# Layer 1's cross attention: the value products of batches 1 to 7 as seven quarter products, with sums on GpSimd

## What is computed

```python
x = x + _L1_xattn_ref(_layernorm(x, axis=-1), ctx_1024, ctx_1024, ...)

def _L1_xattn_ref(Q, K, V, Wq, Wk, Wv, Wo, pre_g, pre_b, ln_g, ln_b):
    D, H, HD, TEMP = 512, 8, 64, math.sqrt(512)
    Qn = _layernorm(Q, pre_g, pre_b)
    Kn = _layernorm(K, pre_g, pre_b)
    q = (Qn @ Wq).reshape(B, Lq, H, HD)
    k = (Kn @ Wk).reshape(B, Lk, H, HD)
    v = (V @ Wv).reshape(B, Lk, H, HD)
    scores = clip(einsum('bqhd,bkhd->bhqk', q, k) / TEMP, -10000.0, 10000.0)
    A = softmax(scores)
    O = einsum('bhqk,bkhd->bqhd', A, v).reshape(B, Lq, D)
    O = _layernorm(O, ln_g, ln_b)
    return O + gelu(O @ Wo)
```

## Time and profile before

| | us |
|---|---|
| runs of the kernel before | 3535.21, 3537.26, 3544.75 (median 3537.26) |
| the profiled execution, own time | 3539.68 |
| its span | 3537.3 |
| PE busy, share of the span | 3102.5, 88% |
| DVE, ACT, POOL busy | 1225.3, 712.7, 392.0 |
| layer 1's cross attention | about 867 to 1204 of the span |
| one regular body (batch) in it | 1008.50 to 1044.37, 35.87 |

### The profile page before, as it was taken

How to read it: one execution, slowest core, us unless ns; L and a number is a source line. 1 busy time by engine, 2 the same in 40 slices (tenths; PEclk the granted TensorE clock), 3 DMA queues, 4 the chain that set the end, 5 groups by cost and what they waited for, 6 DMA issues and landing times. The chain is left out here.

```text
span 3537.3 us, 43385 instructions
## 1 busy us (share of the span) xinstructions
PE 3102.5 (88%) x17505; PEld 1662.7 (47%) x17505; DVE 1225.3 (35%) x2569; ACT 712.7 (20%) x1365; POOL 392.0 (11%) x386
## 2 busy tenths in 40 slices
PE   8998789997899899999889989889998997666666
PEld 5775543333444444344457565436885652111111
DVE  3775430002344569765341132113554310000000
ACT  2443101101232331111012120103452211000000
POOL 4441010001000000001000000004541000000000
PEclk9998889998999999989999999899999999888878
DMA  3110079998111122221540121982002158999999
GB/s 143 45 33 37 13 306 420 406 421 337 62 71 47 37 61 66 101 84 36 207 175 1 45 108 55 376 353 83 24 24 83 77 238 345 420 419 420 420 419 373
DMA packets 103780, 653.65 MB, mean 185 GB/s; under 512 B 20168, under 2 KB 29384, under 8 KB 40648
## 3 DMA queue, kind: packets, MB, share of 16 engines
q1 hardware_dynamic: 98928, 637.67, 44.8%
q0 software_dynamic: 4160, 13.63, 1.0%
q10 hardware_dynamic: 536, 0.14, 0.0%
HBM read 641.89 MB, written 9.50 MB: 184 GB/s over the span
## 5 line engine op out<-in xcount | busy, mean ns | idle before, releaser
L3075 PE MATMUL banks<-ring,h 128*32 128x512 f32 x1024 | 165.2, 754 | 84.5 <-DMA ring<-in_L_ffn_w 61.1
L3058 PE MATMUL banks<-ring,mine 128*32 128x512 f32 x1024 | 167.5, 701 | 51.4 <-DMA ring<-in_L_ffn_w 51.0
L913 PE MATMUL banks<-ring 128*128 128x256 f32 x784 | 179.9, 381 | 0.0
L1839 PE MATMUL banks<-ring,xT 128*64 128x512 f32 x736 | 167.5, 610 | 11.8 <-DMA ring<-in_L_ffn_Wg 5.5
L504 PE MATMUL banks<-normed_features,first 128*128 128x256 f32 x768 | 168.0, 379 | 1.1 <-ACT normed_features L471 1.1
L3186 DVE COPY mine<-mT 128x32 f32<-128x32 f32 x31 | 5.6, 181 | 448.7 <-PE banks L3058 448.7
L913 PEld LDWEIGHTS banks<-ring 128*128 128x128 f32 x784 | 144.5, 190 | 28.7 <-issue 11.4
L429 POOL TENSOR_TENSOR rstd_pairs<-var_eps_pairs,minus_half 128x4 f32<-128x4 f32 x30 | 30.9, 1029 | 1138.7 <-DVE var_eps_pairs L417 961.2
L504 PEld LDWEIGHTS banks<-normed_features,first 128*128 128x128 f32 x768 | 144.6, 190 | 23.0 <-issue 3.2
L3075 PEld LDWEIGHTS banks<-ring,h 128*32 128x32 f32 x1024 | 26.7, 122 | 194.5 <-DMA ring<-in_L_ffn_w 141.9
L886 PE MATMUL banks<-big 128*128 128x512 f32 x256 | 116.9, 602 | 0.0
(11 more groups left out here) (658 smaller groups left out, 5325.7 us busy)
## 6 DMA issues: line engine op xcount, KB each, us to landing
ring<-in_L_ffn_w SPq DMA_DIRECT2D x256, 1024.0 KB, 27.1
ring<-in_L_ffn_Wd SPq DMA_DIRECT2D x24, 2048.0 KB, 23.1
ring<-in_L_ffn_Wg SPq DMA_DIRECT2D x23, 2048.0 KB, 18.8
ring<-in_L_ffn_Wu SPq DMA_DIRECT2D x23, 2048.0 KB, 20.2
wb<-in_L_ffn_W SPq DMA_DIRECT2D x32, 1024.0 KB, 24.5
first<-in_L_ffn_W SPq DMA_DIRECT2D x16, 1024.0 KB, 19.9
second<-in_L_ffn_W SPq DMA_DIRECT2D x16, 1024.0 KB, 22.0
ctxT<-in_ctxT SPq DMA_DIRECT2D x8, 1024.0 KB, 4.9
```

Source lines behind the costliest of these rows:

```text
L913: ins = pe.matmul(halves(n % 2)[:, r, :], a, x, start=(k == 0), stop=(k == 1))
L1839: ins = pe.matmul(ps[H * side:H * side + H, 2 * kind + half, :], xT[:, p % 2, k, H * own:H * own + H], rows_of(where[(name, slot)], C)[:, ...
L3058: ins = pe.matmul(ps[B4 * q:B4 * q + B4, 0, :], mine[:, e % 2, k, :], w[:, q * 512:(q + 1) * 512], start=(k == 0), stop=(k == C - 1))
L3075: ins = pe.matmul(ps[B4 * q:B4 * q + B4, 2, :], h[:, Q * n + q, :], w[:, q * D:(q + 1) * D], start=(n == 0), stop=(n == Q - 1))
```

## The change

In layer 1 too, the values of batches 1 to 7 are made by seven quarter products. The keys stay as they are. In a body the four key units fill steps 0 and 1; step 2 has quarter products 0 to 3, step 3 has 4 to 6. The four turns of the next context follow products 0, 2, 4 and 5. The sums of the value weights and the three copied products lie in `ring`, the buffer that the scan's weights use later; the sums of the context (`csum`) lie in the stage's own space. SP's wait for the values' last unit becomes one for the last quarter product. GpSimd's order becomes: root 0, root 1, the five weight sums, the five sums of context 1, then in each body the root of context b + 2, its five sums, and the four `offsets`; `add_shift` comes after all of it. The value copies of batches 1 to 7 on DVE become joins. Layers 0 and 3 issue what they issued.

```diff
+    KINDS = (1,) if knorm else (0, 1)
+    TURN_AFTER = (0, 2, 4, 5)
...
         def quarters_of(j):
+            if knorm:
+                return range(4 * (j - 2), min(4 * (j - 2) + 4, 7)) if j >= 2 else ()
...
+        def bank_of(par, n):
+
+            return (n + (par if knorm else 0)) % 2
...
                 if not last:
-                    sp.wait_ge(*(multiplied.at(PROD * b + 1) if split else projected.at(UN * b + UN)))
+                    sp.wait_ge(*multiplied.at(PROD * b + 1))
                     sp.dma_start(ctxT[:, par], m.d["ctxT"][b + 2]).then_inc(*ctx_landed[par].up(16))
                     if knorm:
                         sp.wait_ge(*k_turned.at(C * b + 2 * C))
                         sp.dma_start(extra[:], m.d["ctx"][b + 2]).then_inc(*tok_landed.up(16))
...
             def body(b, par, last, step):
                 if last and par == 1:
                     return
-                offsets(b, 1 - par, 0, step)
-                if not last:
-                    mix_context(b + 2, par, step)
-                offsets(b, 1 - par, 1, step)
...
+                if knorm:
+                    if not last:
+                        root_context(b + 2)
+                        mix_context(b + 2, par, step)
+                    offsets(b, 1 - par, 0, step)
...
+            if knorm:
+                root_context(1)
+            for at, kind in enumerate(KINDS):
+                mix_weights(pool, step, (wkb, wvb)[kind], wsum[:, at])
+            mix_context(1, 1, step)
+            run(pool, body, 6 if knorm else 10, pstep)
-            if knorm:
-                with repeat(pool, B) as b:
-                    pool.wait_ge(*var_ready.at(b + 1))
-                    pool.tensor_tensor(m.rstd[:], m.den[:], m.minus_half[:], ALU.pow).then_inc(*rooted.up())
...
+                elif knorm and i < 2:
+                    pe.wait_ge(*k_taken.at(C * b + C + 3 + i))
...
-                    if not end and split:
+                    if not end:
+                        if knorm and j < 2:
+                            for u in range(U * j, U * j + U):
+                                unit(b + 1, 1 - par, u)
                         for n in quarters_of(j):
                             quarter_product(b, par, n)
-                    elif not end:
-                        for u in range(U * j, U * j + U):
-                            unit(b + 1, 1 - par, u)
-                            if knorm and not last and u >= C:
-                                turn_context(b + 2, u - C)
+                            if knorm and not last and n in TURN_AFTER:
+                                turn_context(b + 2, TURN_AFTER.index(n))
...
-def L1_xattn(m, big, rmsw, attn_loads):
+def L1_xattn(m, big, ring, rmsw, attn_loads):
...
+        flat = ring[:].rearrange("p a n -> p (a n)")
+        spare = (flat[:, 0:2560].rearrange("p (i s k n) -> p i s k n", i=1, s=5, k=2),
+                 flat[:, 2560:4096].rearrange("p (s k n) -> p s k n", s=3, k=2))
```

More of the change, by code:

```diff
@@ L709, in cross_attention @@
 def cross_attention(m, oT, qT, hd, scale, wkb, wvb, ctxT, kbias=None, vcol=None, mask=None, clip=None, knorm=None,
-                    ahead=None, inside=None, head=None):
+                    ahead=None, inside=None, head=None, spare=None):
     J = D // hd // 2
@@ L745, in cross_attention @@
                  extra=[P, max(few, 1), SK if few else 1], extraT=[P, C if knorm else 1, SK if knorm else 1],
[L746 to L749, removed]
+                 csum=[P, 2, 3, 2, MIX], bsum=[P, 2], wsum=[P, K2, 5, 2, 1 if spare else MIX],
+                 part=[P, 3, 2, 1 if spare else MIX]) as \
+            (kT, v, qs, pr, prT, sc, col, extra, extraT, csum, bsum, wsum, part), \
+            m.block((o_taken, 1), (turned_taken, TBN), (multiplied, 1), (joined, 4)) as block:
         ps = m.ps
+        if spare:
+            wsum, part = spare
         def ctx_at(par, b):
@@ L827, in mix_context, with offsets @@
                 pool.tensor_tensor(c12, c12, c22, ALU.subtract).then_inc(*mixed.up())
-            def offsets(b, par, kind, step):
-                n, done = 6 * b + 3 * kind, 4 + 8 * b + 4 * kind
+            def offsets(b, par, at, step):
+                kind = KINDS[at]
+                n, done = 3 * K2 * b + 3 * at, 4 + 4 * K2 * b + 4 * at
                 pool.wait_ge(*copied.at(n + 2))
@@ L842, in body, with root_context @@
                     return
-                offsets(b, 1 - par, 0, step)
-                if not last:
-                    mix_context(b + 2, par, step)
-                offsets(b, 1 - par, 1, step)
-            if split:
-                step = Chain(pool, pstep)
-                pool.wait_ge(*w_landed.at(2 * here))
+                if knorm:
[3 more added lines that the diff above has]
+                    offsets(b, 1 - par, 0, step)
+                else:
+                    offsets(b, 1 - par, 0, step)
+                    if not last:
+                        mix_context(b + 2, par, step)
+                    offsets(b, 1 - par, 1, step)
+            def root_context(b):
+                pool.wait_ge(*var_ready.at(b + 1))
+                pool.tensor_tensor(m.rstd[:], m.den[:], m.minus_half[:], ALU.pow).then_inc(*rooted.up())
+            step = Chain(pool, pstep)
+            if knorm:
+                root_context(0)
+            pool.wait_ge(*w_landed.at(2 * here))
+            if not knorm:
                 pool.tensor_tensor(bsum[:], kbias[:, 0:2], kbias[:, 2:4], ALU.add)
[L852 to L855, removed]
             if knorm:
-                with repeat(pool, B) as b:
-                    pool.wait_ge(*var_ready.at(b + 1))
-                    pool.tensor_tensor(m.rstd[:], m.den[:], m.minus_half[:], ALU.pow).then_inc(*rooted.up())
+                root_context(1)
[3 more added lines that the diff above has]
+            run(pool, body, 6 if knorm else 10, pstep)
             if head:
@@ L930, in await_scores @@
                     pe.wait_ge(*q_spread.at(b + 1))
-                    if split and not first:
+                    if not knorm and not first:
                         pe.wait_ge(*joined.at(8 * b))
@@ L1025, in spread, with take_k @@
                    .then_inc(*q_spread.up())
[L1027 to L1029 removed]
+            def take_k(b, par, u, first=False):
+                act.wait_ge(*projected.at(u + 1 if first else C * b + C + u + 1))
+                act.activation(kT[:, par, u, :], ps[:, u % 2 if first else (u + 1 - par) % 2, :], ACT.Identity,
                                bias=0.0 if kbias is None else kbias[:, u:u + 1]).then_inc(*k_taken.up())
             def copy_quarters(b, par, n):
[L1034 removed]
+                at, kind, i = place_of(n)
                 if i > 2:
@@ L1097, in body @@
                         power(b + 1, 1 - par, j + 2 - J)
-                    if not end and split:
+                    if not end:
+                        if knorm and j < 2:
+                            for u in range(U * j, U * j + U):
+                                take_k(b + 1, 1 - par, u)
                         for n in quarters_of(j):
                             copy_quarters(b, par, n)
-                    elif not end:
-                        for u in range(U * j, U * j + U):
-                            if u < C:
-                                take_k(b + 1, 1 - par, u)
-                            elif knorm and not last:
-                                take_context(b + 2, u - C)
+                            if knorm and not last and n in TURN_AFTER:
+                                take_context(b + 2, TURN_AFTER.index(n))
                     if j + 2 < J:
@@ L1208, in body @@
                         norm_context(b + 2, step)
-                    if not end and split:
+                    if not end:
                         for n in quarters_of(j):
                             join_quarters(b, par, n)
-                    elif not end:
-                        for u in range(U * j, U * j + U):
-                            if u >= C:
-                                take_v(b + 1, 1 - par, u - C)
                     if j + 2 < J:
```

75 lines of the change are left out of this document (39 added, 36 removed).

## The result

The changed kernel takes 3560.47 us (median of 6 runs, 3556.09 to 3568.72), the kernel before beside it 3539.19 (6 runs): a ratio of 1.0064 with a 95% interval of 1.0052 to 1.0075, so slower by 21.3 us between medians, where the prediction had 19.8. The profiled execution took 3568.72, the highest of its six; the prediction had some 3559.5 for it.

What follows compares the result with a forecast made beforehand. PE bounds a regular body (35.87 us), with the load-to-key chain 0.37 us behind. Bodies and start sum to +11.0, the slow clock adds 8.8: +19.8, some 3559.5 us profiled, 3557 median; range 3542 to 3567.

Steps and rivals of the forecast that it cites:

- start: Ahead of the first body, DVE's normalizing for context 1 meets GpSimd's weight sums: 3.8 us more, all on the path.
- body 1, without its clock: Body 1: slow token landing of 8.2 us, later load and slowed normalizing, less PE's saving of 1.24: +3.0 us.
- bodies 2 to 4, without their clock: Bodies 2 to 4: the longer chain adds 3.56 us, PE saves 1.24, so 2.3 each, 7.0 for three.
- body 5: Body 5 already had its long normalizing; only the load, 0.43 us later, counts against PE's 1.24: -0.8.
- body 6 and the stage's end: Body 6, which has no context turns, gains PE's saving: -1.6 us.
- clock in bodies 1 to 4: Waits of 1.2 and 2.3 us slow PE's clock; three slow stretches in four places, 2.9 each: +8.8 us.
- The meeting: GpSimd's SBUF sums beside DVE's four normalizing instructions: these take 5.71 us, not 1.91, at start and in bodies 0 to 5.
- The chain's reserve: Load-to-key chain ahead of T2 (turn at j = 2) had 0.37 us to spare; load goes out 0.43 later.
- PE's gain: Seven products for four units save PE 1.69 us a body; a fourth-turn wait of 0.4 to 0.5 leaves 1.24.
- Body 1's landing: Body 1's tokens took 8.20 us in the kernel before; the forecast kept 8.2 for the changed kernel.
- Rival 1: GpSimd's sums don't hold up DVE's normalizing; PE's gain stands and body 5 loses its delay: -15 us, 3522; chance 0.10.
- Rival 2: Sums and normalizing meet but the clock holds, body 5's 2.9 us goes too: +8 us, 3545; chance 0.17.

Runs made afterwards that it cites:

- experiment 2: Changed kernel with GpSimd's context sums after the offsets in each body, and weight sums and context 1's sums ahead of root 1: 3529.09 us, ratio 0.9971.
- experiment 3: Kernel before, still eight value units, with five unused additions on GpSimd behind each root from the second (ten behind the second): 3563.1 us, ratio 1.0067.
- experiment 8: Kernel before with unused GpSimd additions behind the roots, each half as wide (256 columns): 3542.3 us, one run.
- experiment 6: Changed kernel with SP's token load sent ahead of the wait for the products and the ctxT load: 3533.9 us, ratio 0.9983.
- experiment 7: Changed kernel with all sums moved away from L1154 and context turns behind products 0, 1, 2 and 3: 3526.14 us, ratio 0.9965.
- experiment 4: Kernel before with GpSimd's add_shift made to wait until batch 6's attention is done: 3536.27 us, ratio 0.9992.
- experiment 5: Changed kernel with three unused matmuls a body on PE in its waits, in bodies 0 to 5: 3552.93 us, ratio 1.0042.
- experiment 1: Changed kernel with GpSimd's order in a body made root, offsets, sums; start unchanged: 3530.66 us, ratio 0.9971.

## Why the prediction was right

The forecast was 19.8 longer, and 21.3 came. The table sets its steps against the trace. A difference is changed kernel less kernel before; bodies from A to A.

| step | forecast | measured |
|---|---|---|
| start | +3.8 | +4.0 |
| body 0 | -0.4 | +0.1 |
| body 1, without its clock | +3.0 | +1.7 (41.13 - 36.58 = 4.55, less 2.9) |
| bodies 2 to 4, without their clock | +7.0 | +7.1 (15.4 less 3 x 2.77) |
| body 5 | -0.8 | -1.0 |
| body 6 and the stage's end | -1.6 | -1.7 + 1.3 |
| clock in bodies 1 to 4 | +8.8 | +11.2 (2.9 and 3 x 2.77) |
| stage | +19.8 | +22.7 |

- **The meeting** was 5.7 to 5.8 in the start and in the bodies, as body 5 had it. Experiments 2, 3 and 8 show its cause: it goes when the sums go elsewhere (1.92), comes in the kernel before when only sums are added, and shrinks with the addition's length. The Trainium skill (SBUF — State Buffer, "Who interferes with whom") describes an exclusive lock of a port pair for a whole instruction. The trace agrees for DVE, which waits for whole additions. On the size it does not: by the same rule four alternations are 7.4, or 7.0 with the addition's own 1.27, and 5.7 were measured.
- **The chain's reserve.** 0.37 was small enough that the wait at T2 came in each body, and experiment 6 shows the reserve as the lever: with the load some 2.2 earlier against A, the body is shorter than the kernel before's in spite of the same meeting.
- **PE's gain.** T2 to A at full clock is 16.50 in body 0 (977.67 - 961.17), as forecast; bodies in experiment 2 gain 1.20, forecast 1.24; body 6 takes 32.46 for 34.12, 1.66 less, which is what 13.76 - 12.1 gives (the prediction wrote 1.69). The wait at the fourth turn shows as 0.23 in the changed kernel, but the turn starts 0.39 behind the product's end (1055.45 + 1.73 = 1057.18, against 1057.57); experiment 7 gets back 0.45.
- **Body 1's landing, mis-sized.** I carried its 8.2 over; the changed kernel had 6.8 there. It is worth 1.4. The kernels with eight units (before, experiments 3, 4 and 8) all have it in body 1, 8.1 to 8.3; of those with quarter products only experiment 5 has it, in body 2. It goes with the kernel, then, and what makes it is open.
- **The clock, mis-sized.** I counted three slow stretches in four places; it was four, at 2.8 each, and body 5 kept its own. That is 2.4 too little, and the stage's end adds 1.3: there an `attend` took 1.98 that took 1.15 before. In experiment 3 a full count with 2.9 was too much. The prediction took one price from one slow stretch; the price after waits of 2.2 was anything from 0 to 2.9. That idle time is at the root of it experiment 5 shows: filled with matmuls, it costs no clock.
- **Rivals.** Rival 1 is experiment 2, and what parts it from the forecast is the order of GpSimd's stream. Rival 2 would be 3545, the changed kernel with its clock held. Experiment 5 makes that: a stage of +10.2, where rival 2 has +8, and 3552.93 as a whole.
- **Outside the stage** the prediction put nothing. The trace has 6.8 more there, so the profiled execution was 9.2 above the forecast for it, while the medians differ by less than the stage alone. That 19.8 and 21.3 lie so close is in part luck; that the stage's steps do is not.

Open: the whole run gains less than the stage in each kernel that has the changed code and no slow clock in its bodies: 9.4 of 10.8, 11.0 of 15.2, 6.1 of 8.2 and 13.8 of 17.2 in experiments 1, 2, 6 and 7. The traces show where a part of it stands. From the first load of layer 3's cross attention to the first load of the next block these four, and the changed kernel too, take 2.9 to 3.2 more than the kernel before; experiments 3, 4, 5 and 8 take between 0.5 less and 0.3 more. It is two things. PE waits 1.0 to 1.4 for a load of a bias (`bo`) that the kernel before does not wait for, and late in the block the clock is down where it was up:

```profile
2674.11 1.10 PE L980 MATMUL banks<-ring 128*32 128x64 f32 x64 [1.60 <-DVE ring L1201]
```

```profile
2701.51 1.94 PE L1007 MATMUL banks<-ring 128*32 128x64 f32 x64 [1.59 <-DVE ring L1227]
```

The first is the kernel before, at a granted clock of 1.00, the second the changed one, at 0.50; with what follows it costs 1.8. Why experiment 5, which has the changed code, has neither was not tried.

## What to carry to other kernels

When work is moved to an idle engine, look at what stands beside it in time: an idle GpSimd was free, but its SBUF additions behind the very instruction that releases DVE met DVE in every body, and the same additions 9 us earlier cost nothing. A chain with a reserve of tenths turns any such delay into a wait, and a wait of 2 us on TensorE can cost more than its length, because the clock falls behind it; buy the reserve first (an earlier load), then the saving. And measure a saving in the body it is made in: 1.2 us of 1.7 were there all along.

## What the runs showed of the hardware

- The two engines don't share alike. DVE's instruction of 0.48 waits for an addition of 1.27; an addition beside DVE takes up to 1.45, just 0.18 longer. The round is 1.45, not 1.27 + 0.48, so four take 5.7 and not 7.
- The clock fell behind nearly every pair of waits whose second was 2.1 to 2.2, with 1.15 us of work between them (one `attend`), and what it cost between T2 and A varied: 2.9 us in body 5 of the kernel before (waits of 0.80 and 2.19); 2.7 to 2.9 in five of five bodies of the changed kernel (first waits of 1.20 to 1.35), at a granted clock of 0.50 to 0.55 for some 6 us; 2.1, 1.6, 1.6, 1.6 and 0 in experiment 3 (2.21 in body 1, then 0.76 to 0.97). In experiment 8 a first wait of 0.18 was enough for 1.6:

```profile
987.26 1.15 PE L996 MATMUL banks<-big 128*64 128x64 f32 x32 [0.18 <-DVE big L1217]
990.60 0.63 PE L1013 MATMUL banks<-identity,big 128*128 128x128 f32 x4 [2.19 <-ACT big L1045]
...
1009.95 1.15 PE L996 MATMUL banks<-big 128*64 128x64 f32 x32
```

- Behind a single wait at T2 of 0.68 (body 1 before), 1.05 or 1.41 (body 0 of experiment 6 and of the changed kernel) T2 to A was at full clock.
- In experiment 5 matmuls for nothing in the waits kept the clock at 1.00, also in body 2, where 1.84 and 0.27 of waiting were left. They cost nothing and gave back 2.7 to 2.9 us a body.
